# Two attention layers on one core: the second attention's weighting in eight slots and four batches, with the sums of the weights shared out differently between VectorE, GpSimd and TensorE

## What is computed

```python
q = layernorm(q_x, g_q, b_q) @ Wq.T            # 16 heads of 32
k, v = layernorm(kv_x, g_kv, b_kv) @ Wkv.T     # 3202 keys
attn = softmax(einsum('bhqd,bhkd->bhqk', q, k) * 32 ** -0.5)
out = einsum('bhqk,bhkd->bhqd', attn, v)       # 4096 x 512
x = q_x + out @ Wo.T + bo
x = x + silu(x @ W1.T + b1) @ W2.T + b2
```

## Time and profile before

| | us |
|---|---|
| median of 3 runs (lowest, highest) | 5529.31 (5528.18, 5532.56) |
| the profiled execution, its own time | 5531.83 |
| span of its instructions | 5529.7 |
| first score of the second attention, to the first of its last item | 1874.3 to 4623.2 |

### The profile page before, as it was taken

One profiled execution on the slowest core, in us unless ns is written; L12 is line 12 of the kernel. 1 busy time (PEld: TensorE's weight loads), 2 busy tenths in 40 slices (PEclk: granted clock), 3 DMA queues, 4 the chain that ended last, 5 costly groups with the idle time before them and its releaser, 6 DMA issues. The chain is left out here.

```text
span 5529.7 us, 93901 instructions
## 1 busy us (share of the span) xinstructions
PE 5310.5 (96%) x28684; PEld 3343.9 (60%) x28684; DVE 4009.0 (72%) x6947; ACT 3173.3 (57%) x5792; POOL 2329.5 (42%) x1156
## 2 busy tenths in 40 slices
PE   8989999999699799999999999999999996999999
PEld 7744444444377466666666666666666663787777
DVE  6589999999577688888888888888888885332331
ACT  4258888888433366666666666666666664322222
POOL 0000000000000388888888888888888885000000
PEclk9989999999899799999999999999999998999999
DMA  7521111111343311111111111111111111322220
GB/s 216 129 46 37 39 38 38 38 38 32 112 120 111 102 41 29 40 41 41 36 34 39 42 41 35 34 40 42 41 32 36 41 30 61 114 92 69 92 84 23
DMA packets 329591, 324.44 MB, mean 59 GB/s; under 512 B 185744, under 2 KB 193808, under 8 KB 327184
## 3 DMA queue, kind: packets, MB, share of 16 engines
q1 hardware_dynamic: 329232, 319.92, 21.8%
HBM read 219.18 MB, written 100.53 MB: 58 GB/s over the span
## 5 line engine op out<-in xcount | busy, mean ns | idle before, releaser
L426 DVE TENSOR_REDUCE a_maxes<-a_mscore 128x1 f32<-128x458 f32 (+4 forms) x5376 | 3037.8, 625 | 599.0 <-PE a_mscore L485 566.9
L409 ACT ACTIVATE a_prob<-a_score 128x512 f32<-128x512 f32 x4992 | 2635.7, 598 | 1184.4 <-PE a_score L494 1171.2
L494 PE MATMUL a_score<-a_q,a_k 97*128 97x512 f32 (+1 forms) x4992 | 1975.6, 430 | 11.6 <-ACT a_prob L409 7.9
L485 PE MATMUL a_mscore<-a_k,a_qm 96*128 96x458 f32 (+4 forms) x5376 | 1892.3, 415 | 53.7 <-DMA a_k<-k 52.4
L513 PE MATMUL a_acc<-a_prob,a_v 128*32 128x512 f32 x9984 | 1593.6, 601 | 0.0
L485 PEld LDWEIGHTS a_mscore<-a_k,a_qm 96*128 96x128 f32 (+1 forms) x5376 | 1475.0, 310 | 177.0 <-issue 54.0
L375 POOL TENSOR_TENSOR a_added<-a_added,a_prob 128x1024 f32<-128x1024 f32 x640 | 1527.3, 2386 | 71.0
L494 PEld LDWEIGHTS a_score<-a_q,a_k 97*128 97x128 f32 (+1 forms) x4992 | 916.0, 193 | 966.5 <-ACT a_prob L409 524.8
L372 POOL TENSOR_TENSOR a_added<-a_prob 128x1024 f32<-128x1024 f32 x128 | 305.1, 2383 | 1893.5 <-ACT a_prob L409 1879.6
L508 PE MATMUL a_acc<-a_prob,a_ones 128*1 128x512 f32 x2048 | 960.9, 591 | 0.0
L513 PEld LDWEIGHTS a_acc<-a_prob,a_v 128*32 128x32 f32 x9984 | 291.8, 108 | 297.7 <-issue 153.2
(11 more groups left out here) (205 smaller groups left out, 3878.0 us busy)
## 6 DMA issues: line engine op xcount, KB each, us to landing
a_qm<-q SPq DMA_DIRECT2D x384, 64.0 KB, 1.9
a_q<-q SPq DMA_DIRECT2D x384, 64.0 KB, 1.9
acc<-a_acc_sb SPq DMA_DIRECT2D x384, 64.0 KB
e_part<-acc SPq DMA_DIRECT2D x90, 256.0 KB, 3.4
a_k<-k SPq DMA_DIRECT2D x48, 416.0 KB, 6.2
q<-m_qout SPq DMA_DIRECT2D x128, 128.0 KB, 2.3
e_wo<-wo_split SPq DMA_DIRECT2D x32, 512.0 KB, 4.1
k<-kv_k1out SPq DMA_DIRECT2D x24, 512.0 KB, 2.9
```

The costliest lines, as they stand in the source:

```text
L409: act.activation(prob[:, t], score[SCORES[it.j][t]][:], ACT.Exp, scale=SCALE).then_inc(exp_done, 1)
L426: dve.tensor_reduce(maxes[j][:, t, c:c + 1], mscore[u % UNIT_BANKS][:, 0:wide], AX.X, ALU.max).then_inc(unit_read, 1)
L485: pe.matmul(mscore[u % UNIT_BANKS][:, 0:wide], qm[j][r:r + ROW, t:NB:NB // P], kt[kk][r:r + ROW, at:at + wide], start=True, stop=True).the ...
L494: pe.matmul(score[SCORES[it.j][t]][:], kt[it.k][r:r + C, i * P:(i + 1) * P], qt[it.j][r:r + C, :], start=True, stop=True).then_inc(score_d ...
```

## The change

The second attention's weighting has eight slots in four batches of two. Group 3 now takes part in the values: in slots 0 and 1 it holds tiles 3 and 7, so these two slots have four tiles each, and slots 2 to 7 have three. Groups 0 to 2 and the ones in slots 2 to 7 are as before in kind; the ones now sum tiles 8, 9, 23, 24 and 25 and `total`. Since rows 96 to 127 of the accumulator hold a fourth partial result until the ones start there with slot 2, ScalarE copies them to a tile `side` before tile 20 (`copy_side`), batch 1 waits for this copy, and SyncE stores it with the rest: `SIDE` is 4. VectorE adds tiles 2 to 4 and tiles 5 to 7 within their own item, each in two pieces of 256 columns, at tiles 9, 10, 17 and 19 of the item. GpSimd adds the pairs (0,1)+(10,11), 12, 14, 16, 18, 20, then tile 22, then VectorE's two sums (1024 columns), then the two halves. Batches and the copy stand at other tiles. `ending` loads and adds four partials, and puts `total` and half of the inverted sums into tiles that are free at the time.

```diff
-            self.ROWS, self.SIDE, self.SUMS = 128, 3, 1
-            self.slots = [[(0, 3 * i), (1, 3 * i + 1), (2, 3 * i + 2), (3, ("one", 3 * i))] for i in range(8)]
-            self.slots.append([(0, 24), (1, 25), (3, ("sum", None))])
-            self.batches = [[0, 1], [2, 3], [4, 5], [6, 7], [8]]
-            self.at = {3: (3, True), 9: (4, True), 14: (0, False), 19: (1, False), 25: (2, False)}
-            self.copy_at = 5
+            self.ROWS, self.SIDE, self.SUMS = 128, 4, 1
+
+            self.slots = [[(c, 4 * i + c) for c in range(4)] for i in range(2)]
+            for i in range(2, 8):
+                first = 8 + 3 * (i - 2)
+                what = [("one", 8), ("one", 9), ("one", 23), ("one", 24), ("rest", 25), ("sum", None)][i - 2]
+                self.slots.append([(0, first), (1, first + 1), (2, first + 2), (3, what)])
+            self.batches = [[0, 1], [2, 3], [4, 5], [6, 7]]
+            self.at = {9: (2, True), 13: (3, True), 17: (0, False), 22: (1, False)}
+            self.copy_at, self.side_at = 14, 20
+
+            self.sum_at = (9, 10, 17, 19)
...
-            more = dict(enumerate([2, 1, 1, 0, 1, 2, 1, 1, 1, 0, 1, 2, 1, 1, 1, 1, 1, 2, 1, 1, 1, 1, 2, 1, 1, 0]))
+            more = dict(enumerate([1, 1, 1, 0, 2, 1, 2, 0, 1, 1, 2, 1, 1, 0, 1, 1, 2, 1, 2, 0, 2, 1, 1, 1, 2, 0]))
...
-ADDS = 9
-ON_VECTOR, PIECES = range(22, 25), 4
-READ_BY = 7
+
+ADDS, READ_BY, SUMS_READ = 9, (1, 2, 5, 7), 8
+ON_VECTOR, PIECES = (range(2, 5), range(5, 8)), 2
+VSUMS = len(ON_VECTOR) * PIECES
...
+                if APART:
+                    sp.wait_ge(side_copied, n + 1)
+                    sp.dma_start(acc_out[ATEND, bass.ds(h * hd, hd), cols], side[3 * 32:P, :]).then_inc(side_stored, 16)
...
-                for i in range(1, 7):
-                    pool.wait_ge(exp_done, it.n * ST + 3 * i + 3)
-                    if i == 1:
+                for i, t in enumerate((10, 12, 14, 16, 18, 20)):
+                    pool.wait_ge(exp_done, it.n * ST + t + 2)
+                    if i == 0:
                         if not it.first:
                             pool.wait_ge(add_done, base)
-                        pool.tensor_tensor(added[:], prob[:, 1:3], prob[:, 4:6], ALU.add).then_inc(add_done, 1)
+                        pool.tensor_tensor(added[:], prob[:, 0:2], prob[:, 10:12], ALU.add).then_inc(add_done, 1)
                     else:
...
+                pool.tensor_tensor(added[:, 0], added[:, 0], prob[:, 22], ALU.add).then_inc(add_done, 1)
+                pool.wait_ge(vsum_done, it.n * VSUMS + VSUMS)
                 pool.wait_ge(add_done, base + 7)
+                pool.tensor_tensor(added[:], added[:], vsum[:], ALU.add).then_inc(add_done, 1)
+                pool.wait_ge(add_done, base + 8)
                 if not it.first:
 
                     pool.wait_ge(pv_done, it.n * NBATCH)
                 pool.tensor_tensor(total[:], added[:, 0], added[:, 1], ALU.add).then_inc(add_done, 1)
-                pool.wait_ge(add_done, base + 8)
-                pool.wait_ge(vsum_done, it.n * PIECES + PIECES)
-                pool.tensor_tensor(total[:], total[:], vsum[:], ALU.add).then_inc(add_done, 1)
...
+            def copy_side(n):
+
+                act.wait_ge(pv_done, n * NBATCH + 1)
+                act.wait_ge(side_stored, n * 16)
+                act.activation(side[3 * 32:P, :], acc[3 * 32:P, :], ACT.Copy).then_inc(side_copied, 1)
...
-            def add_up(n, i):
-
+            def add_up(n, first, which, i):
+
+                tiles = ON_VECTOR[which]
                 if i == 0:
-                    dve.wait_ge(exp_done, n * ST + ON_VECTOR[-1] + 1)
-                    dve.wait_ge(add_done, n * ADDS)
+                    dve.wait_ge(exp_done, n * ST + tiles[-1] + 1)
+                    if which == 0 and not first:
+
+                        dve.wait_ge(add_done, n * ADDS - ADDS + SUMS_READ)
...
+                if b == 1 and APART:
+                    pe.wait_ge(side_copied, n + 1)
```

More of the change, by code:

```diff
@@ L126, in __init__ @@
         self.opens = {min(ts): b for b, ts in enumerate(tiles)}
-        self.closes = [max(ts) for ts in tiles]
+        summed = [[t[1] for i in b for _, t in self.slots[i] if isinstance(t, tuple) and t[0] != "sum"]
+                  for b in self.batches]
+        self.closes = [max(ts + ones) for ts, ones in zip(tiles, summed)]
         self.units_at, made = [], 0
@@ L229, in attention @@
         LOADS = 16 * 3 * HALVES
[L230 removed]
+        ATEND = 3 if APART else SIDE
+        STORED = 16 * (ATEND + SUMS)
         def items(eng):
@@ L461, in _ @@
                             maximum(it.n + 2, it.j, it.use + 1, u)
-                    if APART and t < PIECES and not it.first:
-                        add_up(it.n - 1, t)
-                if APART and it.last:
-                    for i in range(PIECES):
-                        add_up(it.n, i)
+                    if APART and t in L.sum_at:
+                        add_up(it.n, it.first, *divmod(L.sum_at.index(t), PIECES))
             if weights:
@@ L503, in weigh @@
                     for c, what in L.slots[i]:
-                        after = [x for later in L.slots[i + 1:] for x, _ in later if x == c]
+                        kind = lambda x: isinstance(x, tuple)
+                        same = [j for j, slot in enumerate(L.slots) for x, w in slot if x == c and kind(w) == kind(what)]
+                        start, stop = i == same[0], i == same[-1]
                         if isinstance(what, tuple):
+                            keys = LAST_KEYS if what[0] == "rest" else P
                             if what[0] == "sum":
                                 pe.wait_ge(add_done, n * ADDS + ADDS)
-                            mm = pe.matmul(acc[c * 32:c * 32 + 1, :], ones[:],
-                                           total[:] if what[0] == "sum" else prob[:, what[1]],
-                                           start=(i == 0), stop=not after)
+                            mm = pe.matmul(acc[c * 32:c * 32 + 1, :], ones[0:keys],
+                                           total[:] if what[0] == "sum" else prob[0:keys, what[1]],
+                                           start=start, stop=stop)
                             continue
@@ L513, in weigh @@
                         mm = pe.matmul(acc[c * 32:c * 32 + 32, :], vt[kk][:, L.FIRST[half] + at, :],
-                                       prob[:, what], start=(i == 0), stop=not after)
+                                       prob[:, what], start=start, stop=stop)
                 mm.then_inc(pv_done, 1)
@@ L1196, in ending @@
         h = [sb(f"h{i}", [P, NB], F32) for i in range(2)]
+        total = h[1]
+        assert H * T // P == NB
         hh = [sb(f"hh{i}", [P, NB], F32R) for i in range(2)]
@@ L1222, in part_of, with recip_part @@
             return part, 0, 2 + (n - 1) * KT + k
+        def recip_part(n, k):
+            return h[0][:] if n == 0 and k % 2 else part[:, SIDE]
         @block.sync
```

45 lines of the change are left out of this document (21 added, 24 removed).

## The result

The change made the kernel slower: 5602.7 us (median of 4 runs, 5600.9 to 5606.0) against 5530.9 us for the kernel before on the same chip; the ratio is 1.0128, 95% interval 1.0113 to 1.0144. The profiled execution has a span of 5604.0 us, 74.3 us longer than that of before.

A forecast was written before the change was run, and what follows sets the result against it. TensorE's issue of products was taken as the bound. From the profiled 5531.8 us, -114 for 127 beats, +5 at the attention's end and +3.5 at the next stage gave 5426, 5424 for the median; range 5376 to 5495.

The forecast's parts named there:

- What bounds the kernel: Second attention: TensorE's issue of products is what an item takes, a beat of 21.66 us before the change.
- the count of crossings: TensorE, per item: four batch crossings, their following steps and 46 plain steps make 20.39 us, a floor 1.19 us lower.
- a slot with four tiles: Second attention's batches: a slot with four tiles of values costs no more than one with a column of ones.
- The rest of the beat: Second attention, 13 tiles between batches: 0.4 us of stalls from ScalarE and VectorE, bounds 0 and 1.2; beat 20.76 us.
- VectorE's sums: Second attention: four new sums of 768 elements an item at 0.9 us each, bounds 0.50 and 1.0.
- the third rival: Second attention: VectorE's sums stop GpSimd and TensorE waits for `total`; 5823 us if fully; chance 0.08.
- the rule weighed with it: Shared SBUF interfaces of GpSimd and VectorE: one-input sums are free for GpSimd; the tail of the attention pays.
- rivals 2 and 3: GpSimd bounds the beat (5480 us; 0.14 with mixtures), or VectorE's sums stop GpSimd (5823 us; 0.08).
- Rival 4: Second attention: the slot isn't saved, a batch's time being set by something else, and the ends cost 8; 5537 us; chance 0.03.
- End of the attention: Last item: the split of W1 on VectorE slows GpSimd's chain, `total` near 38 us, stage end near 43.5: +5 us.
- Start of the last stage: Before its first product: one more addition of 0.71 us a quarter and one more load a group, +3.5 us, bounds 2 and 6.
- Later blocks hide it beside TensorE: Last stage after its start: the fourth partial's extra load and addition are hidden beside TensorE, so no cost counted.

The follow-up runs named there:

- e10: e1 with VectorE's four sums an item cut from 256 to 32 columns each, the other columns left out of the sums; 5463.4 us.
- e2: The changed kernel with GpSimd's fourth addition cut from 1024 to 128 columns, the product over 2 rows kept; 5601.9 us.
- e12: e11 with the order of the three score banks turned at tile 10 in the second attention; about 5417 us.
- e1: The changed kernel with tile 25's summing product over all 128 rows, against a column of ones in rows 0 and 1 and zeros below; 5470.9 us.
- e6: e1 with the last stage reading three partials, the fourth written but left out of the output; 5443.8 us.
- e11: e8 with the last stage's sums one hidden tile later and the split of W1 held until GpSimd's last sum is done; 5435.7 us.
- e13: The kernel before with only the last stage's sums of partials one hidden tile later; 5527.3 us.
- e8: e1 with partials 1 to 3 and the inverted sums of the next quarter loaded earlier in the last stage; 5464.6 us.
- e3: The kernel before with tile 18's product with ones over 2 rows instead of 128; 5645.6 us.
- e4: e1 with the product of tile 25 over 64 rows; 5604.0 us.
- e5: e1 with the product of tile 25 over 96 rows; 5470.3 us.

## Why the prediction was wrong, step by step

The forecast was 5424 us and the range 5376 to 5495; the time is 5603.

- **What bounds the kernel: right.** TensorE's issue of products sets the beat, before and after. e10 shows that VectorE does not, e2 that GpSimd does not.
- **The step that failed** is the count of crossings, "Four crossings: 4 x 2.17 + 4 x 0.34 + 46 x 0.225 = 20.39 us", with the sentence on a slot with four tiles behind it. It took all batches to be alike. I asked whether four tiles of values in a slot cost more than three and a column of ones, found a row for it, and was right on that: batch 0, sixteen such products, takes its 2.17 us. I did not ask the same of the other new form, ones over 2 rows. Before, tile 25 was in a slot only with its values, over 128 rows (zeros below), and its sum was GpSimd's, where an addition over 2 rows takes what one over 128 rows does (1.27 and 1.29 us). No row of the trace shows a product of this form, so by my own rule it wanted a bound from both sides: hidden beside its slot, 0, or a slot of its own, about 1 us or 127 us in all. With it the high end would have been 5495 + 127 = 5622, and the measured time inside. The page of the Trainium skill named above would have suggested this rival. What the runs showed in its place: one crossing of 3.25 us and three of 2.17, 1.08 us an item or 137 us in all. Mending that one product takes the time to 5471 us, inside the range.
- **The rest of the beat: right in kind, 0.14 us short.** Without the short product it is 20.90, forecast 20.76. The stall of 0.4 us in the stretch of 13 tiles is 0.5. Of the two causes that I added up, VectorE's load has no part in it (e10) and ScalarE's pace is likely but not tested; 0.17 us is a third, a bank reused after two scores (e12), which in the kernel before lay under the batch at tile 25. That the sum came so near is in part luck. (20.39 + 0.4 is 20.79; the 20.76 that I wrote is 4 us too low over the stage.)
- **VectorE's sums:** 1.03 us each, forecast 0.9 and bounded by 1.0. Too low, without effect.
- **GpSimd:** seven additions and two in 20.1 us, forecast 20.3; its 1.9 us of idle time an item is the longer beat. In e1 it idles 0.75 us an item, and `total` is ready 1.7 us ahead of its product, forecast 1.4. No addition grew beside VectorE's longer sums (2381 ns mean, before 2386), so the third rival is refuted and the rule weighed with it held.
- **The place of the loss** was named by rivals 2 and 3, the batch at tile 13, for another reason. Their sign for the reader was a wait of TensorE behind `total`; there is none. Rival 4 (no slot is saved) comes nearest in effect, but not in cause: a batch's time is still set by its slots, and the batch at tile 13 has three.
- **End of the attention:** forecast +5, measured +9.1. The mechanism is there and was sized too small: beside the split GpSimd's five additions of 1024 columns take 18.5 us, where 12.3 is usual, and the last three 3.1 to 3.2 us each. `total` is ready 40.5 us after the item's first score, where I had 38, and from there to the next stage it is 6.8 us, where I had 5.5. From the trace of the change:

```profile
4674.60 18.51 POOL L391 TENSOR_TENSOR a_added<-a_added,a_prob 128x1024 f32<-128x1024 f32 x5
...
4693.26 3.12 POOL L394 TENSOR_TENSOR a_added<-a_added,a_prob 128x512 f32<-128x512 f32 x1
...
4696.53 3.14 POOL L397 TENSOR_TENSOR a_added<-a_added,a_vsum 128x1024 f32<-128x1024 f32 x1
...
4699.74 3.19 POOL L402 TENSOR_TENSOR a_total<-a_added 128x512 f32<-128x512 f32 x1
```

- **Start of the last stage:** +4.8, forecast +3.5, inside its bounds of 2 and 6.
- **"Later blocks hide it beside TensorE": wrong, 21 us.** I named the work that hides the fourth partial but not the queue. The load, the sum and the split of a quarter pass through one buffer in turn, and the split of the hidden values stands behind them on VectorE. The waits of the last stage of the kernel before show that the cover was used up: VectorE already waited up to 7.8 us for the first quarter, and TensorE 1.3 us a block. The fourth partial made that 3.0 us and brought the falls of the clock; without it (e6) the blocks take 102.8 us instead of 105.1.

## What to carry to other kernels

When products are packed side by side in column groups, give them all the same height of the array: pad a short one with zero weights. Here a product over 2 rows beside ones over 128 cost 1.08 us, and the 126 rows of zeros cost nothing. When a change brings an operation in a form that the trace of before does not have, that form is an unknown cost, even if it does less work. And a wait on an engine's queue costs what is queued behind it: here moving the waiting instruction later took TensorE's wait away (e11, e13), and making most of its input come sooner did not (e8).

## What the runs showed of the hardware

- A product over 2 or over 64 rows does not run beside products over 128 rows in other column groups; over 96 rows it does. Each such product added 1.08 us to a batch of 2.17 (the change and e3 with 2 rows, e4 with 64; e5 with 96 and e1 with 128 added nothing).
- A wait of TensorE of 2.9 us in otherwise full work was followed by a fall of the granted clock, seen as 1.37 us for four products of the last stage where 0.93 is usual. TensorE's full speed is 2.4 GHz, and the lower of its two levels 1.2 GHz. Of the 2.9 us a block that the fourth partial cost, some 1.2 to 1.4 were this.
- A reduction on VectorE over 768 elements of SBUF in a partition takes 1.03 us, over 96 elements 0.26, and GpSimd's additions beside such sums keep their 2.38 us. Beside the split of W1 (casts and subtractions over 2048 elements) an addition of 512 columns on GpSimd takes 3.1 to 3.2 us instead of 1.3, and VectorE's subtraction 4.3 instead of 2.3 (the change against e11, where the two no longer overlap).
